# A vision tower with a routed feed-forward on one core: the routed sums go into one table that is the output itself, the patch sums move to VectorE behind earlier pixel loads, and the steps of the tower are listed in another order

## What is computed

```python
h = tok(x)                                    # 16x16 patches of the image and 4 shifted copies: layer norm, einsum
h = h + attn0(layernorm(h))                   # 12 heads, token i > 0 does not attend to itself
h = h + ffn0(layernorm(h))                    # z = the normed h; z += attention; z += MLP
                                              # images 32 to 63: gumbel-weighted sum over three sub-widths
h = h + attn1(layernorm(h))                   # differential attention over the 12 heads of a token
h = h + ffn1(layernorm(h))                    # routed: 2 of 4 groups and 4 of 8 experts in each, 8 of 32 a token
# ffn1: sum over experts e of gate[n, e] * (gelu(x @ W1[e] + b1[e]) @ W2[e] + b2[e])
```

## Time and profile before

| | before |
|---|---|
| median of 3 runs | 859.93 us (858.62 to 863.21) |
| profiled execution | 855.93 us, its span 854.1 us, mean granted TensorE clock 0.88 |
| TensorE matmuls | 716.3 us busy, 84% |
| VectorE | 409.5 us, 48% |
| GpSimd | 330.0 us, 39% |
| ScalarE | 233.3 us, 27% |
| chain that ended last | TensorE 64%, VectorE 17%, DMA 8%, issue 6% |

### The profile page before, as it was taken

How to read it: one execution, slowest core, us unless ns; L and a number is a source line. 1 busy time by engine, 2 the same in 40 slices (tenths; PEclk the granted TensorE clock), 3 DMA queues, 4 the chain that set the end, 5 groups by cost and what they waited for, 6 DMA issues and landing times.

```text
span 854.1 us, 19282 instructions
## 1 busy us (share of the span) xinstructions
PE 716.3 (84%) x6418; PEld 606.3 (71%) x6418; DVE 409.5 (48%) x1119; ACT 233.3 (27%) x670; POOL 330.0 (39%) x274
## 2 busy tenths in 40 slices
PE   3886785859987999785555999999999999999991
PEld 3882564636574579675434989998999999999991
DVE  4967445574468512798582333333333333333330
ACT  2201221212323430111321333333333333333330
POOL 3843104320102330052202455545545555556552
PEclk9986696868896789897856999999999999999996
DMA  8940000000000002000512575546454566455334
GB/s 192 236 102 0 2 3 1 3 1 2 2 1 0 1 1 112 1 1 1 156 40 78 151 220 154 121 132 159 103 154 106 157 170 191 113 155 135 72 45 94
DMA packets 36571, 71.94 MB, mean 84 GB/s; under 512 B 6646, under 2 KB 22743, under 8 KB 36503
## 3 DMA queue, kind: packets, MB, share of 16 engines
q0 software_dynamic: 16048, 18.49, 12.7%
q10 hardware_dynamic: 8352, 34.30, 11.7%
q1 hardware_dynamic: 12119, 18.41, 8.0%
HBM read 60.33 MB, written 12.44 MB: 85 GB/s over the span
## 4 chain that ended last, share of the span: by engine, by line
PE 64%; DVE 17%; DMA 8%; issue 6%; POOL 2%; ACT 2%; SPq 1%; DVEq 0%; POOLq 0%
PE bank L1449 14%; PE bank L1441 11%; PE bank L1444 7%; DMA arena<-normed_rows,fetch_u 5%; PE bank L1229 4%; DVE v_space L822 4%; PE bank L1342 4%; PE bank L1426 3%; PE bank L1303 3%; PE bank L1249 3%; PE bank L1318 2%; PE bank L1267 2%; PE bank L1277 2%; PE bank L1296 1%; PE bank L1330 1%
## 5 line engine op out<-in xcount | busy, mean ns | idle before, releaser
L625 POOL DMA_INDIRECT summed<-arena,number_u x80 | 127.2, 1590 | 28.2 <-issue 25.0
L621 POOL DMA_INDIRECT arena<-normed_rows,fetch_u x80 | 78.3, 979 | 140.4 <-DMA arena<-normed_rows,fetch_u 72.3
L1158 DVE COPY arena<-bank 128x256 f32<-128x256 f32 x81 | 34.4, 424 | 154.4 <-PE bank L1426 154.4
L794 ACT ACTIVATE arena<-bank,arena 128x128 f32<-128x128 f32 x234 | 64.6, 375 | 117.0 <-PE bank L1444 117.0
L1449 PE MATMUL bank<-arena 128*128 128x192 f32 x468 | 82.9, 326 | 0.7 <-DVE arena L1178 0.7
L537 POOL TENSOR_SCALAR rstd<-mv 128x4 f32<-128x4 f32 x12 | 2.8, 230 | 195.6 <-DVE mv L861 195.6
L1449 PEld LDWEIGHTS bank<-arena 128*128 128x128 f32 x468 | 75.4, 190 | 1.0 <-issue 1.0
L1441 PE MATMUL bank<-arena 128*128 128x128 f32 x468 | 60.0, 278 | 0.9
L565 POOL TENSOR_TENSOR arena<-arena,v_space 128x2304 f32<-128x2304 f32 x8 | 34.5, 4315 | 67.5 <-DVE arena L1106 56.3
L1441 PEld LDWEIGHTS bank<-arena 128*128 128x128 f32 x468 | 56.5, 192 | 5.2 <-issue 5.2
L1178 DVE TENSOR_SCALAR arena<-bank,arena 128x192 f32 x80 | 33.4, 418 | 54.4 <-PE bank L1449 52.7
(11 more groups left out here) (227 smaller groups left out, 1305.6 us busy)
## 6 DMA issues: line engine op xcount, KB each, us to landing
arena<-in_moe_w_dram ACTq DMA_DIRECT2D x15, 579.0 KB, 5.8
arena<-in_moe_w_dram ACTq DMA_DIRECT2D x15, 576.0 KB, 4.4
w_space<-in_moe_w_dram ACTq DMA_DIRECT2D x7, 579.0 KB, 5.1
w2small<-in_moe_w_dram ACTq DMA_DIRECT2D x7, 579.0 KB
w_space<-in_moe_w_dram ACTq DMA_DIRECT2D x7, 576.0 KB, 3.7
wab<-in_moe_w_dram ACTq DMA_DIRECT2D x7, 576.0 KB
arena<-in_xf_dram SPq DMA_DIRECT2D x8, 480.0 KB, 13.7
arena<-in_w_dram SPq DMA_DIRECT2D x8, 450.0 KB, 12.1
```

Source lines behind the costliest of these rows:

```text
L621: pool.indirect_dma_start(out=mo_stage[:, s * ROWN:(s + 1) * ROWN], out_offset=None, in_=normed_rows, in_offset=bass.IndirectOffsetOnAxis( ...
L625: pool.indirect_dma_start(out=summed[s], out_offset=bass.IndirectOffsetOnAxis(ap=number_u[:, s:s + 1], axis=0), in_=mo_res[:, s * D:(s + 1 ...
L794: nc.scalar.activation(mo_hT[:, m, :], bank[2 + m][:, 0:P], ACT.Gelu, bias=b1[:, m:m + 1]).then_inc(free[2 + m], 1)
L1158: nc.vector.tensor_copy(mo_xT.rearrange("p k t -> p (k t)"), bank[1][:, 0:2 * P]).then_inc(free[1], 1)
```

## The change

**One table.** `summed` is gone. `out` gets 128 more rows for padding, and every tile adds into it. As neighbours of different experts may now meet in a row, a tile waits until all tiles before its expert's first have landed. The count for every tile is made on VectorE and TensorE into `landed` (behind the table), and GpSimd loads one number of it in each turn. The zero fill and both closing transfers go. The two padding accumulates of GpSimd follow one another.

**Tokenization.** `betasum` becomes one 120x192 row sum, made by VectorE in five more instructions a chunk between those of `weff`; the semaphore waits are for the instruction two back. GpSimd keeps only `foldsum`. The first wait is for a lot of three (`gamma5`, `beta5`, `cnt`); the other constants are loaded behind all pixels, the router's six behind the weights. In the last chunk TensorE does half of the tiles to their end first, with one `betasum` product where there were five.

**Order.** The list of steps is permuted (lines of it below).

```diff
-        ("tok", "T", 0), ("ln", "A", 0), ("xT", "A", 0), ("tok", "T", 1), ("qk", "A", (0, 0)), ("ln", "A", 1), ("bias", "A", 0), ("qk", "A", (0, 1)),
+        ("tok", "T", 0), ("ln", "A", 0), ("tok", "T", 1), ("xT", "A", 0), ("qk", "A", (0, 0)), ("bias", "A", 0), ("ln", "A", 1), ("qk", "A", (0, 1)),
...
-        ("V", "A", 0), ("av", "A", (0, 0)), ("V", "A", 1), ("av", "A", (0, 1)), ("front", "A", (1, 0)), ("av", "A", (0, 2)), ("qk", "A", (1, 1)),
-        ("front", "A", (1, 1)), ("av", "A", (0, 3)), ("av", "A", (0, 4)), ("av", "A", (0, 5)), ("ln", "z", 0), ("ln", "B", 0), ("back", "A", (1, 0)),
...
+        ("V", "A", 0), ("av", "A", (0, 0)), ("V", "A", 1), ("av", "A", (0, 1)), ("av", "A", (0, 2)), ("av", "A", (0, 3)), ("qk", "A", (1, 1)),
+        ("av", "A", (0, 4)), ("av", "A", (0, 5)), ("front", "A", (1, 0)), ("ln", "z", 0), ("front", "A", (1, 1)), ("ln", "B", 0), ("xT", "B", 0),
...
+        ("av", "A", (1, 3)), ("av", "A", (1, 4)), ("gumbel", "B", 0), ("av", "A", (1, 5)), ("av", "B", (0, 0)), ("av", "B", (0, 1)), ("ln", "z", 1),
+        ("av", "B", (0, 2)), ("ln", "B", 1), ("av", "B", (0, 3)), ("xT", "B", 1), ("qk", "B", (1, 0)), ("av", "B", (0, 4)), ("qk", "B", (1, 1)),
...
+        ("D", "D", (0, 6)), ("norm", "R", 0), ("D", "D", (1, 1)), ("D", "D", (1, 2)), ("D", "D", (1, 3)), ("D", "D", (1, 4)), ("gates", "R", 0),
+        ("D", "D", (1, 5)), ("D", "D", (1, 6)), ("begin", "R", 0), ("norm", "R", 1), ("gates", "R", 1), ("slots", "R", 0), ("slots", "R", 1),
         ("counts", "R", 0), ("begin", "R", 1), ("table", "R", 0),
...
             def fold_sums():
-                loaded(pool, "const")
                 for c in range(FC):
-                    pool.wait_ge(sem(f"in_pixels{c}"), 32)
-                    link(tt(out=betaprod if c else betasum, in0=w5[:, c], in1=repeat(beta5[:, :, c], 2, D), op=ALU.mult))
-                    if c:
-                        link(tt(out=betasum, in0=betasum, in1=betaprod, op=ALU.add))
                     pool.wait_ge(sem("weff"), c + 1)
...
             with pool.Fori(0, pairs) as pair:
                 for s in range(2):
                     i = pair * 2 + s
+                    settled = pool.value_load(landed[0:1, bass.ds(i, 1)], min_val=16, max_val=8 * MAXT + 16)
...
                     pool.wait_ge(free[0], result)
                     pool.sem_inc(sem("adding"), 1)
-                    pool.indirect_dma_start(out=summed[s], out_offset=bass.IndirectOffsetOnAxis(ap=number_u[:, s:s + 1], axis=0),
+                    pool.wait_ge(sem(f"accumulated{1 - s}"), settled)
+                    pool.sem_inc(sem("adding"), 1)
+                    pool.indirect_dma_start(out=out, out_offset=bass.IndirectOffsetOnAxis(ap=number_u[:, s:s + 1], axis=0),
                                             in_=mo_res[:, s * D:(s + 1) * D], in_offset=None, compute_op=ALU.add).then_inc(sem(f"accumulated{s}"), 16)
-            pool.wait_ge(sem("out_begun"), 16)
-            pool.wait_ge(sem("accumulated1"), pool.snap(pairs * 16 + 16))
-            pool.sem_inc(sem("adding"), 1)
-            pool.dma_start(out=out.rearrange("(p t) d -> p (t d)", p=P), in_=summed[1][0:TOK, :].rearrange("(p t) d -> p (t d)", p=P),
-                           accum_op=ALU.add, max_dma_last_dim=6 * D * 4).then_inc(sem("out_stored"), 16)
...
+                for v in range(NSH):
+                    if v:
+                        ins = stt(out=weff[:, c, 0:D], in0=w5[:, c, v, :], scalar=gamma5[:, v, c:c + 1], in1=weff[:, c, 0:D], op0=ALU.mult, op1=ALU.add)
+                    step[0] += v < NSH - 1
+                    ins.then_inc(sem("weff" if v == NSH - 1 else "dve_step"), 1)
+                    if c or v:
+                        dve.wait_ge(sem("beta_step"), c * NSH + v)
+                        ins = stt(out=betasum, in0=w5[:, c, v, :], scalar=beta5[:, v, c:c + 1], in1=betasum, op0=ALU.mult, op1=ALU.add)
...
                     if v < NSH - 1:
-                        link(ins)
-                ins.then_inc(sem("weff"), 1)
+                        dve.wait_ge(sem("dve_step"), step[0])
...
+                link(stt(out=first_f[:, 0:NE], in0=tiles_f[:, 2, :], scalar=numbers[:, 0:1], in1=tiles_f[:, 1, :], op0=ALU.is_le, op1=ALU.mult))
+                nc.vector.reduce_sum(first_f[:, NE:NE + 1], first_f[:, 0:NE], AX_X).then_inc(sem("first_tiles"), 1)
```

130 lines of the change are left out of this document (77 added, 53 removed), and 20 rows, old and new, of the table NEG.

## The result

The changed kernel takes 848.28 us (median of 4 runs, 844.44 to 851.02) against 860.74 us for the kernel before beside it: ratio 0.9845, interval 0.9817 to 0.9872, or 12.5 us less. The forecast was 831, 29 us less. The profiled execution of the changed kernel took 850.15 us with a span of 848.3; that of the kernel before took 855.93 with a span of 854.1, so between the two profiles only 5.8 us lie.

The account below looks back on a forecast made before the run. It took VectorE to bound tokenization and router, mutual waits the tower, TensorE the loop. Tokenization -10.5, order -6.5, router -6, loop +1.5 and tail -7.5 gave -29 from 859.93: 831 us, range 816 to 848.

Parts of the forecast that it names:

- Tokenization: Start to VectorE's first read of the banks: -11.9 us, or -8.5 if two blocks fall to half clock; -10.5 taken.
- Order: Tower: the permuted steps shorten waits around the layer norms, -6.5 us in all, bounds +3 and -15.
- (a): Tower: `front A 1` behind the `av` steps starts the first pair of layer norms earlier, -2.5 us.
- (b): Tower: two more `av B` steps lie inside the second pair of layer norms, 5.95 - 2.1 = -4 us.
- (c): Tower: `fc2` closes up by one `av`, less VectorE's share ahead of the norm, -1.4 us.
- (d): Tower: `fc1 M (1, 0)` ahead of `D (0, 1)` saves a TensorE stall but delays ScalarE's exponentials and copies, +1.4 us.
- A: Rival for tower and router: the order gives nothing and the router -3, time 843 us; chance 0.15.
- Router: Router: second half's gates start about 11.6 us earlier, first half's `slots` cost VectorE 6.6; -6 us, bounds -11 and 0.
- Loop: Tile loop: register load and wait hidden under TensorE's 4.6 us a tile; +1.5 us, between 0 and +16.
- C: Rival in the loop: a register load above 1.0 us makes GpSimd's turn the bound, 845 us; chance 0.07.
- D: Rival in the loop: the ordering wait makes GpSimd the bound, 53 us more, time 882 us; chance 0.06.
- Tail: After the last scatter: closing copy and accumulate go, -7.5 us, not less than 6 or more than 8.

Follow-up runs that it names:

- after_again: The changed kernel, unchanged, run again beside the kernel before on one chip: 837.91 us, ratio 0.9803.
- after: The changed kernel as first measured and profiled: median 848.28 us, ratio 0.9845 to the kernel before; profiled execution 850.15 us.
- order_only: The kernel before with only the changed kernel's list of steps: 857.62 us, ratio 1.0028.
- before_third: The kernel before, unchanged, profiled again: 856.67 us, ratio 1.0009.
- old_order: The changed kernel with the whole list of steps of the kernel before: 843.56 us, ratio 0.9790.
- pad_old_attention: The changed kernel with 32 idle instructions at VectorE's start and the steps from `front A (1, 0)` to `ln z 1` in the old order: 847.34 us, ratio 0.9851.
- pad_after: The changed kernel with 32 idle instructions at the start of VectorE's program: 846.70 us, ratio 0.9834.
- router_alt: The changed kernel with `begin R 0` behind the second half's gates and the first half's slot counting ahead of the second half's logits: 831.16 us, ratio 0.9733.
- delay: The changed kernel with six idle semaphore instructions on GpSimd ahead of the ordering wait: 837.62 us, ratio 0.9808.
- fourth group: Four runs beside the kernel before on one chip: both kernels unchanged, the new tokenization alone and the new order alone; the kernel before took 855.59 us.
- third group: Four runs beside the kernel before on one chip: that kernel again and three variants of the changed one; the kernel before took 855.49 us.
- pad_before: The kernel before with 40 idle instructions at the start of VectorE's program: 861.49 us, ratio 1.0003.
- pad_two_tables: two_tables with 32 idle instructions at the start of VectorE's program: 849.48 us, ratio 0.9884.
- two_tables: The changed kernel with the two tables, zero fill and both closing transfers of the kernel before, without load or ordering wait: 851.30 us, ratio 0.9882.
- first, second and fifth: Three groups of runs, each beside the kernel before on one chip; that kernel took 860.72, 860.77 and 861.33 us.

## Why the prediction was too low, step by step

**Tokenization (forecast -10.5): right.** It measured -11.9, the term's first number, from the same steps: VectorE at 8.1, first block at 11.19 (11.8 in the forecast), blocks 4.40 apart (4.55), first read at 48.33 (48.3). That the total meets the forecast to 0.1 us is luck. The first block with its squares took 7.35 us (11.19 to 18.54) where 6.4 stood, and the piece from the last chunk to the read 3.4 where 2.8 stood; the earlier start and the six shorter blocks gave that back. (Ten additions at 0.445 are 4.45 us, not 4.3, still under 4.55.) A first read at 52 came too, in three of the fifteen profiles with the new tokenization. Timeline of `after_again`:

```profile
11.20 5.48 PE L1204 MATMUL bank<-v_space,arena 120*128 120x193 f32 x16 [11.20 <-DVE v_space L813]
16.48 3.41 PE L1208 MATMUL bank<-cnt,arena 120*128 120x1 f32 x16
19.75 5.10 PE L1204 MATMUL bank<-v_space,arena 120*128 120x193 f32 x16
24.68 1.84 PE L1208 MATMUL bank<-cnt,arena 120*128 120x1 f32 x16
26.38 2.86 PE L1204 MATMUL bank<-v_space,arena 120*128 120x193 f32 x16
```

Its second block takes 5.10 where the next takes 2.86, and TensorE waited for nothing in between. The first read is at 51.8 there, about the -8.5 of the second case, but not in its way. That case had later blocks fall back in clock; here the slow pace of the start lasts longer. This profile's record of the granted clock begins at 24.30 us, with 1.00, just where the pace rises (at 17.23 in `after`); what was granted before that is not recorded. By the Trainium skill, "TensorE: Matmul & The Clock Gate", section "HAM oscillation — how this bites in real kernels", a TensorE kept busy stays at full clock. All fifteen profiles agree from that first record on: it is 1.00 up to the first read of the banks.

**Order (-6.5): this term failed.** The tower takes 289.9 to 298.4 us in the profiles with the new list and 295.6 to 297.1 in those with the old one, so -1.4 in the mean, with 8.5 us of spread among those with the new list (289.9 and 296.4 for the changed kernel itself). `order_only` against `before_third`, both counted from their first read of the banks (0.9 later in `order_only`), shows step by step where it goes. (a) is right and more: the first transposes behind the pair of norms start at 139.34 against 142.30:

```profile
139.34 2.63 PE L1218 MATMUL bank<-ident,zx 128*96 128x128 f32 x8 [5.81 <-DVE zx L880]
```

```profile
142.30 2.63 PE L1218 MATMUL bank<-ident,zx 128*96 128x128 f32 x8 [8.36 <-DVE zx L880]
```

The first fence is `order_only`, the second `before_third`. The wait is 2.5 shorter and the norm's output 3.9 earlier. But at `ln z 1` the lead is gone (+1.7), and at the second `ln B` the new list is 2.0 *behind*. At `ln M 0`, with every `av B` step of the first half done in both lists, they are level (0.0; -0.6 in `after` against `old_order`), where (a) and (b) together had -6.5. So (b) took back what (a) had gained. It had charged 2.1 us for VectorE's share of an `av` step ahead of the norm. `pad_old_attention` shows the price: there two `av B` steps stand between `ln z 1` and `ln B 1` and the two are 10.5 us apart, in `pad_after` one step and 6.1. That is 4.4 for one more step ahead of the norm, double the charge. Which waits make up the rest was not tried apart. (c) and (d) come out near nothing: `ln M 1` +2.5, `ln D 1` -1.0, the router's norm -1.0. Putting the old order of that part back gains nothing either: the first norm output is 3.5 us later than in `pad_after`, the second 2.6, and the median 0.6 us above it, inside the intervals. Of the rivals, A (the order gives nothing, 0.15, with the time 843) was the nearest in its mechanism.

**Router (-6): this term failed.** It measured +2.0. The step that failed is "with begin 0 and the logits on TensorE directly behind, gates of half 1 start about 11.6 us earlier". The 48 products do run early. But "directly behind" assumed that what follows them takes no longer than before. I priced neither the wait for VectorE nor the clock of that stretch. The 48 products end 12.4 us earlier against `norm R 0`; 3.0 are lost in the wait for the residual add behind VectorE's gates, and 6.4 because TensorE's work from there on (the eight pairs of `begin R 0`, the transposes and the logits above all) ran at 0.50 instead of 1.00. The pairs take 7.56 us at 0.50 in all ten profiles with the new list that have them ahead of the logits, and 4.23 at 1.00 in five of the six with the old one. So the gates gained 3.0. The `slots` in VectorE's line cost 6.6 as priced. `router_alt` shows how much of it lies in the order: with the logits ahead of `begin R 0`, and the first `slots` in VectorE's wait for them, the router takes 92.7 in place of 98.3 (`delay`, same chip), and the median is 831.16 in place of 837.62, though all of it still runs at 0.50. Whether the full clock alone would give the 6.4 back was not tried.

**Loop (+1.5): right where no copy is held, wrong where copies are, by a term that was not in the sum.** In the fourth group it is nothing: 375.8 against 376.1. The load takes 0.29 + 0.16 us in GpSimd's queue, where I took 0.4, and lies ahead of the scatter's landing. Rivals C and D are false: C needs over 1.0 us for the load, and D has 53 us of ordering waits, which come to 10.2 in all. The chain of the kernel after in the loop:

```profile
502.96 0.29 POOLq L604
...
503.27 0.16 POOLq L604
...
503.63 6.88 DMA out_dram<-arena,number_u
```

In the other groups copies are held, with one table or two, with or without the load; only the two kernels that start the scatter later have few. What I took for a cost of the change was mostly a difference between two profiles: that of before has no held copy and at 855.93 lies with the 855.5 of the third group, that of after has 29. Between two profiles that both hold copies the 13.0 us shrink to 4.9 (`pad_after` against `pad_before`). Against `pad_two_tables` one table adds 7.1 us to the loop, which eats most of the 9 of the tail. The waits of GpSimd in the kernel after, from 450 to 838 us (who waits for whom: us, times, longest):

```profile
POOL arena L612 <- DMA out_dram<-arena,number_u: 54.2, 15, 5.8
POOL out_dram L618 <- DMA out_dram<-arena,number_u: 10.2, 20, 3.3
```

L618 is the ordering wait. It is no longer than in `after_again` (9.7 us, 16 times; L612 there 58.2), where nothing is lost, so these waits do not show where the 7 us go. That a held copy makes rows late, and so the next scatter, is only argued.

**Tail (-7.5): right in kind, 1.4 too small**: -8.9 here and 19.6 - 10.6 = 9.0 in the fourth group. The last scatter begins 3.6 us after the last copy, as before (834.70 and 838.19 there), but the span ends 848.3 - 841.3 = 7.0 us after that, where the forecast had 4.56 + 0.4 + 3.4 = 8.4. The 3.4 that follow a last landing, or the landing, were too dear, and the upper bound of 8 too low.

**The sum.** In the fourth group, if the parts add up: tokenization -9.0, order +2.0, table -10.7 (of it tail -9.0), total -17.7. From -29 it comes like this: the order gave 14.5 less than the 12.5 forecast (-12.5 to +2.0), the tokenization 1.5 less, and the table 4.7 more (-10.7 against -7.5 + 1.5), so -29 + 14.5 + 1.5 - 4.7 = -17.7. The first pair of kernels has 5 us less again (-12.5); held copies under one table are the difference that its profile shows.

**What holds the copies stays open.** Five theories went: the register load (`two_tables`), the place in VectorE's program (`pad_after`), the change itself (`pad_before`), chance from one execution to the next, and the chip. Against chance: the profiles go by group, held in the first, second and fifth (with the two kernels that start the scatter later nearly free of it) and none at all in the eight of the third and fourth. Against the chip: the third and the fifth group have the same chip number, and one has none, the other 29. (If that number does not name the same piece of hardware both times, this last point falls; the record does not say.) What remains is some condition that lasts through a group; with it the kernel before takes 860.7 to 861.3, without it 855.5 to 855.6. By the Trainium skill, "SBUF — State Buffer", section "🔬 SBUF: two separate sides", VectorE and GpSimd share one pair of ports, and VectorE holds it in its two-port mode or with two SBUF inputs; by "VectorE: DVE Perf Modes", section "Why PSUM operands drop a tier", a copy out of PSUM uses no such mode. By that a copy from a bank is not held by a scatter. The 0 of 276 cases in the third and fourth group agree; the 29 of 34 in the kernel after, and the like in the others, do not.

## What to carry to other kernels

When a step is moved ahead on one engine, write down every engine's own list around it: the gates waited for logits, the logits stood behind eight pairs of products that nobody was waiting for, and these behind a residual add that had got behind the other half's gates. A price taken from a row holds for that row's clock: the same products cost 4.23 us at 1.00 and 7.56 at 0.50. Compare two kernels' profiles only when both were taken in one group; here a difference of 13 us in the loop came mostly from profiles taken under different conditions. A second table that only saves an ordering wait was worth less than its closing transfers: they cost 9 us, the single table's loop nothing without held copies and 7 us with them.

## What the runs showed of the hardware

- A VectorE copy from PSUM (128x256, f32, 0.42 us) starts only as a GpSimd indirect DMA instruction (1.59 us) ends in 27 to 33 of 34 to 42 cases in some groups of runs, and never in 276 cases in others; groups under one chip number show both. The kernel before takes 860.7 to 861.3 us with it and 855.5 to 855.6 without, the changed one 846.7 (padded) to 848.3 and 837.9. What makes the condition is not known.
- A register load by GpSimd from SBUF takes 0.29 + 0.16 us.
- TensorE's second block can be slow without idle time before it (5.10 against 2.86 us), in three of the fifteen profiles with the new tokenization and in `pad_before`. In these the record of the granted clock begins only behind it (24.30 us in `after_again`, against 17.23 in `after`), so a window ahead of that says nothing of the clock.
